# Transposing and copying the next group's first expert rows ahead of the attention's transposed rows

## What is computed

```python
xn = layernorm(x)
# attention of one batch, 16 heads of depth 8
q = elu((xn @ Wq + bq) @ Wq2 + bq2) + 1; k = the same with Wk; v = (xn @ Wv + bv) @ Wv2 + bv2
S = einsum('bhld,bhle->bhde', k, q)
out = einsum('bhmd,bhde->bhme', v, S) / (einsum('bhld,bhld->bhl', q, k) + 1e-6)
attn = layernorm(xn + out @ Wo + bo) * gamma + beta
# experts
shared = (x1 * silu(x2)) @ shared_w2.T            # x1, x2 = split(xn @ shared_w1.T)
buf[e, rank] = xn[token]                          # up to 160 rows for an expert
h = buf @ expert_w1.T; y = (h1 * silu(h2)) @ expert_w2.T
combined[token] += gate * y
result = x + attn + shared + combined
```

## Time and profile before

| what | value |
| --- | --- |
| time, median of 3 runs | 367.81 us (367.22 to 368.82) |
| time of the profiled execution | 367.13 us |
| span of the profiled execution | 365.3 us |
| PE busy, share of the span | 325.1 us, 89% |
| PEld | 307.3 us, 84% |
| DVE | 279.4 us, 76% |
| POOL | 246.6 us, 67% |
| ACT | 196.2 us, 54% |

### The profile page before, as it was taken

The page is one execution under the profiler, slowest core; times in us unless marked ns, Lnnn a source line. Parts: engine busy times, 40 slices in busy tenths (PEclk is TensorE's granted clock), DMA queues, the critical chain, the costliest instruction groups (busy, mean ns, idle before and its releaser), DMA issues.

```text
span 365.3 us, 8486 instructions
## 1 busy us (share of the span) xinstructions
PE 325.1 (89%) x2765; PEld 307.3 (84%) x2765; DVE 279.4 (76%) x1083; ACT 196.2 (54%) x432; POOL 246.6 (67%) x205
## 2 busy tenths in 40 slices
PE   1799957789999999999999999999999999998910
PEld 0789956779999999999999999999998999998800
DVE  3888797868777868888787888888787878746384
ACT  3567727145747465665747465665737475643200
POOL 3142874355778788787878878788888777888210
PEclk9989988889999999999999999999999999999985
DMA  7999654921587878878886878778777878863859
GB/s 224 333 355 294 236 125 104 307 66 31 129 213 174 196 198 194 200 177 220 192 209 156 206 198 199 209 159 232 188 197 162 204 189 191 210 127 30 251 168 299
DMA packets 57739, 70.78 MB, mean 194 GB/s; under 512 B 12544, under 2 KB 45568, under 8 KB 57696
## 3 DMA queue, kind: packets, MB, share of 16 engines
q1 hardware_dynamic: 40032, 55.68, 50.1%
q0 software_dynamic: 15552, 13.51, 22.7%
q10 hardware_dynamic: 2112, 1.05, 1.0%
HBM read 54.78 MB, written 15.43 MB: 192 GB/s over the span
## 4 chain that ended last, share of the span: by engine, by line
PE 79%; DVE 6%; DMA 4%; issue 3%; ACT 3%; POOL 2%; SPq 1%; DVEq 0%; POOLq 0%
PE bank L1147 28%; PE bank L1157 11%; PE bank L1081 11%; PE bank L1090 5%; PE bank L1186 4%; PE bank L1166 3%; PE bank L1192 2%; DVE x_sb L1009 2%; PE bank L1044 2%; PE bank L1199 2%; DMA gath<-xng,idx_g 2%; DMA x_sb<-in_x 2%; PE bank L1207 2%; PE bank L1223 2%; PE bank L1121 1%
## 5 line engine op out<-in xcount | busy, mean ns | idle before, releaser
L446 POOL DMA_INDIRECT acc<-ys,idx_g x64 | 102.8, 1606 | 29.9 <-issue 15.5
L1147 PE MATMUL bank<-xe,ew 128*128 128x160 f32 x768 | 117.1, 302 | 1.0 <-ACT xe L554 0.6
L1147 PEld LDWEIGHTS bank<-xe,ew 128*128 128x128 f32 x768 | 108.3, 191 | 2.3 <-ACT xe L554 0.8
L427 POOL DMA_INDIRECT gath<-xng,idx_g x80 | 81.7, 1021 | 30.9 <-issue 22.6
L512 ACT ACTIVATE si<-bank 128x480 f32<-128x480 f32 (+1 forms) x96 | 52.0, 542 | 58.9 <-PE bank L1147 36.7
L685 DVE TENSOR_TENSOR ac<-si,bank 128x480 f32<-128x480 f32 x64 | 41.2, 644 | 19.6 <-ACT si L512 13.5
L1081 PE MATMUL bank<-xT,shw 128*128 128x128 f32 x384 | 53.8, 294 | 0.1
L1157 PE MATMUL bank<-ew,ac 128*128 128x128 f32 x384 | 53.4, 275 | 0.4 <-issue 0.4
L1157 PEld LDWEIGHTS bank<-ew,ac 128*128 128x128 f32 x384 | 49.5, 192 | 1.6 <-issue 0.8
L1081 PEld LDWEIGHTS bank<-xT,shw 128*128 128x128 f32 x384 | 49.9, 207 | 0.7 <-issue 0.4
L1090 PE MATMUL bank<-shw,acs 128*128 128x128 f32 x192 | 28.1, 283 | 8.2 <-DVE acs L676 5.8
(11 more groups left out here) (139 smaller groups left out, 558.5 us busy)
## 6 DMA issues: line engine op xcount, KB each, us to landing
ew<-in_expert_w SPq DMA_DIRECT2D x64, 384.0 KB, 3.5
ew<-in_expert_w SPq DMA_DIRECT2D x64, 192.0 KB, 3.3
ew<-acc SPq DMA_DIRECT2D x8, 512.0 KB, 5.2
x_sb<-in_x SPq DMA_DIRECT2D x8, 256.0 KB, 6.8
xng<-xn SPq DMA_DIRECT2D x8, 256.0 KB, 4.9
acc<-betas SPq DMA_DIRECT2D x4, 512.0 KB, 5.6
acc<-zeros SPq DMA_DIRECT2D x4, 512.0 KB, 4.9
gath<-xng,idx_g POOLq DMA_INDIRECT x80, 3.4
```

Of the source, the lines that this page charges most:

```text
L427: pool.indirect_dma_start(out=gath[:, p, m, :], out_offset=None, in_=xng, in_offset=bass.IndirectOffsetOnAxis(ap=idx_g[:, g % 4, m:m + 1], ...
L446: pool.indirect_dma_start(out=acc[adds_to[g, m]], out_offset=bass.IndirectOffsetOnAxis(ap=idx, axis=0), in_=src, in_offset=None, compute_o ...
L1147: last = pe.matmul(h_view(n, half_ + 1, CAP)[:, c, :], ew[p][m][:, k * P:(k + 1) * P], xe[:, p, m, :], start=True, stop=True)
```

## The change

In the main loop `first_rows(g + 1)` on PE is called right behind `up(g, 3)`, ahead of `out_T(a)` and `down(g, 2)`, where it had stood behind `down(g, 2)`. On ACT `first_copy(g + 1)` is called right behind the silu of `up(g, 3)`, ahead of `out_copy` and `y_copy(g, 2)`, where it had stood behind both. DVE, POOL and SP keep their order. No instruction, wait or count is added or taken away.

```diff
@@ ACT
                 silu(('e', g, 3))
+                if g + 1 < NG:
+                    first_copy(g + 1)
                 if attend:
                     out_copy(g + 1)
                 y_copy(g, 2)
-                if g + 1 < NG:
-                    first_copy(g + 1)
@@ PE
                 up(g, 3)
+                if g + 1 < NG:
+                    first_rows(g + 1)
                 if a < B:
                     out_T(a)
                 down(g, 2)
-                if g + 1 < NG:
-                    first_rows(g + 1)
                 if a < B:
                     out_projection(a)
                 shared_down(EARLY + g)
```

## The result

| | before | after |
| --- | --- | --- |
| time, median of 7 runs each, on one chip | 368.41 us (367.22 to 369.47) | 370.9 us (369.99 to 371.91) |
| ratio after to before | | 1.0068, 95% interval 1.0051 to 1.0086 |
| profiled execution, its span | 367.13 us, 365.3 us | 370.2 us, 368.3 us |
| PE busy | 325.1 us | 327.9 us |
| loop: first to last start of L1179, a transpose that PE runs once in each group | 244.32 us | 249.64 us |

The change costs 0.0068 x 368.41 = 2.5 us, 1.9 to 3.2. The whole interval lies above 1, and above the 0.5% that the prediction took as the least that can be told apart, so the kernel is slower, though by less than 1%.

A forecast was written before the change was run, and what follows sets the result against it. The prediction took PE to bound the main loop. Stalls of 0.32 us in 15 groups, 4.8 us, less 1.2 us of gather waits, gave +3.6 us on 367.81 us: 371.4 us, range 369.5 to 374.0.

The forecast's parts named there:

- PE sets the pace, and the earlier copies bring nothing: Main loop: PE is busy 16.35 of 16.35 us a group; the copies were already in time by 0.27 us.
- ACT's copies: ACT, group's end: L553 starts 0.53 us after the transposes begin; L554 delays L597 by 0.16 us if they overlap.
- The projection's wait: PE at L1223: its weight load waits for ACT's L597 and begins 0.28 to 0.35 us late.
- The shared down product's wait: PE at L1090: its weight load waits for the later y_copy and begins 0.26 to 0.33 us late.
- Which chain decides: PE, group's end: the waits of projection and shared down product are not added; the larger counts.
- 0.32 us a group, 15 times: PE in groups 0 to 14: the stall taken for each group, 4.8 us in all.
- 1.18 us given back: Group 11: PE's two gather waits, 0.31 and 0.44 us, should go, and with them the group's extra 1.18 us.
- The sum, +3.6 us: Whole kernel: 4.8 us of stalls less 1.2 us from the gather waits that go.
- (a): Rival, not slower: the projection starts in time and only gathers are waited for; 368.1 to 368.6 us, 11%.
- (b): Rival, faster: only group 11's two gather waits go, with no stall in their place; 366.6 us, 3%.
- (c): Rival, much slower: each new stall lowers PE's clock for the next up product; 14 us more, 385 us, 2%.
- (d): Case of PE's stall at its upper end, 0.46 us a group; 373.5 us, or 374.7 if the gather waits stay.

The follow-up runs named there:

- one_ahead: Kernel before with only the rest tile's transpose moved on PE to right behind the up product of expert 3, ACT's order kept; 371.91 us, ratio 1.0030.
- pe_only: Kernel before with only PE's part of the change, the three transposes moved, ACT's order kept; 367.04 us, ratio 1.0092.
- y_chain: Kernel before with PE's down product of expert 2 behind the next group's transposes, and ACT's y_copy behind the first rows' copies; 366.94 us, ratio 1.0106.
- after_again: The changed kernel, unchanged, profiled a second time on another chip; 366.03 us, ratio 1.0077 to the kernel before.
- gathers_early: Kernel before with only POOL's order changed: gathers of slots 1, 2 and 3 each ahead of a scatter they stood behind; 392.91 us, ratio 1.0632.
- before_third: The kernel before, unchanged, profiled a third time, on the third chip; 370.00 us, ratio 1.0022.
- act_only: Kernel before with only ACT's part of the change, the first rows' copies ahead of the other two, PE's order kept; 383.80 us, ratio 1.0361.

## Why the prediction was right

Forecast 371.4 us in 369.5 to 374.0; measured 370.9. Part of that closeness is luck: the forecast was set on 367.81 us, the median of three runs of before, and the median of seven is 368.41. The forecast difference was +3.6 us, the measured one +2.5.

- **PE sets the pace, and the earlier copies bring nothing.** Right. Every kernel that held PE up grew by just that in each group: 0.11, 0.33, 0.40, 1.17 us. "No idle time at all" was read from modelled ends: PE waited 0.02 us at L1090 in the groups of before too.
- **The transposes' own cost, 3 x 0.11 us at either place.** Right, and one_ahead shows the single 0.11.
- **ACT's copies.** L553 0.53 us after the transposes' start: exactly (189.53 to 190.06). L554 0.16 us ahead of L597: exactly (190.34 to 190.50). So two short copies and a longer one behind them overlap as the two shown pairs did.
- **The projection's wait.** 0.28 to 0.35 us late at the value chosen: 0.30.
- **The shared down product's wait.** 0.26 to 0.33 us: 0.33, its upper end. Here a term was mis-sized. The hand-off from ACT to the weight load was bounded by 0.04 and 0.11 us, and the lower end of the stall used the 0.04, which gave this chain 0.07 us of slack. In before it was 189.98 - 189.87 = 0.11 at this very pair, and it is 0.11 to 0.12 us there in every kernel in which L1090 waits; from L597 to L1223 it is 0.05 us in every kernel in which L1223 waits. The rows on hand had the answer: a load that starts just 0.11 us after its producer, where 0.11 is the shown price of the hand-off, is a load that waited, even if no idle time is printed. "0.26 us stays even if ACT were faster" is therefore 0.33.
- **Which chain decides.** The text said the larger counts; pe_only and y_chain show that the `y_copy` chain alone gives all of it. The projection's wait, the one that the weight loads show best, is nearly beside the point: without it the group is no shorter. In after PE is 0.30 us late at L1223 and 0.05 us more at L1090 (0.16 us between the loads where 0.11 is the least); less the 0.02 us that before had there, that is the 0.33. So undoing only the order on ACT brings nothing back, which is pe_only. Undoing only the place of the attention's transposes wasn't run by itself.
- **0.32 us a group, 15 times.** Measured 0.33 in 14 intervals and 0.32 in the last.
- **1.18 us given back.** Right in after_again, pe_only and y_chain: groups of 16.68 us in place of 17.5 to 17.6. In the first execution of after group 11 was 17.37 us with no wait for a gather in it, but with ACT late as in group 7.
- **The third transpose of group 7 in time by 0.05 us.** It didn't wait in after_again, where POOL had 2.2 us more by then, so the 0.05 us wasn't put to the test.
- **The end.** The adds on DVE begin 19.80 us after the last L1179 in both kernels (330.68 to 350.48, 334.47 to 354.27), so the loop's shift arrives in full at these adds.
- **The sum, +3.6 us.** The loops give 248.04 - 244.65 = +3.4 and 248.04 - 244.32 = +3.7. The second takes before's loop from its first profile, on a chip with a higher time of before (368.41 against 363.26 us). The medians give +2.5 (1.9 to 3.2), +2.8 for after_again, +3.8 and +3.7 for pe_only and y_chain, whose loops are as long as after_again's. So a comparison of medians here is good for some 0.5 to 1 us, and the first interval lies a little under what the loop says. The stage ahead of the loop alone differs by up to 2.1 us between profiles from one chip. What of the rest is chance and what isn't stays open.

Of the rivals, (a) needed a stall under 0.20 us and a projection in time: it is late in every group. (b) fell with it. (c), a clock that falls, is refuted twice, with 0.22 and with 1.15 us of idle time in each group at a granted clock of 1.00. (d), 0.46 us, asked for copies that don't overlap; they do.

## What to carry to other kernels

In a loop that one engine bounds, small work of that engine between a producer and the consumer of its copied result costs its own duration if it is moved away and the chain has no slack, even where no idle time is printed in front of the consumer. To see whether there is slack, compare the end of the copy with the start of the consumer's weight load: if the gap is the bare hand-off of that pair (0.11 us from L565 to L1090, 0.05 us from L597 to L1223), the load was already waiting. The distance between the loads says the same: 0.13 us where 0.11 is the least. An engine whose busy time looks moderate may be full through its pauses: count instructions times (duration plus pause), and don't reorder such a queue without asking which transfer's landing its present order hides.

## What the runs showed of the hardware that was not expected

- A result of PE can be seen late by its waiters, up to 3.8 us after its recorded end, and then by several waiters at one instant (ACT and SP's queue at 174.62 and 174.56 in gathers_early; at 207.00 and 206.93 in after). It comes on some chips and in some executions, in the unchanged kernel too: 10.3 us of such waits at L572 and L512 in before_third. With a chain without slack it hits the time at once: 0.70, 0.21 and 0.69 us in the first execution of after.
- Executions of kernels that are the same up to the loop reach its first L1179 at 82.39 to 84.47 us on the first chip of the experiments, and at up to 87.07 us on the others.
- A scatter that the program lets wait for the landing of the last one but one waited up to 1.6 us when no gather stood between the three (11 times in the loop of gathers_early), and 3 times, up to 0.8 us, in the loop of before. The first of three in gathers_early landed by 4.66 us after POOL began it.
- With 1.15 us without a weight load in each group of 17.52 us (act_only) the granted clock stayed at 1.00.
- The time from the end of an ACT copy to the weight load that waits for it keeps its size at a given pair of instructions over all kernels, but isn't the same for each pair: 0.11 us from L565 to L1090, 0.05 us from L597 to L1223.
